# Building a graph adjacency matrix: who takes the window sums out of PSUM and adds them

## The reference, cut to what matters

```
dst = sorted(...)                       # 20000 destinations, denser at low numbers
count[s, d]     = sum over edges e of (src[e] == s) * (dst[e] == d)
adjacency[s, d] = sum over edges e of (src[e] == s) * (dst[e] == d) * edge_weight[e]
```

## Time and profile before

| | |
|---|---|
| median of 3 runs | 3178.88 us (3175.09 to 3182.57) |
| the profiled execution | 3182.64 us, its span 3180.9 us |
| mean granted TensorE clock | 0.901 |
| the stage `build_adjacency` | from 0 to 267.24 us, where the next stage's first load is issued |
| its windows | from 23.3 us on (first `first_hot`); TensorE's last matmul ends at about 252.65 us |

### The profile page before, as it was taken

How to read it: one execution, slowest core, us unless ns; L and a number is a source line. 1 busy time by engine, 2 the same in 40 slices (tenths; PEclk the granted TensorE clock), 3 DMA queues, 4 the chain that set the end, 5 groups by cost and what they waited for, 6 DMA issues and landing times. The chain is left out here.

```text
span 3180.9 us, 40026 instructions
## 1 busy us (share of the span) xinstructions
PE 2602.6 (82%) x14620; PEld 2308.1 (73%) x14621; DVE 2000.4 (63%) x2885; ACT 1356.1 (43%) x2206; POOL 358.5 (11%) x309
## 2 busy tenths in 40 slices
PE   5774878887986968984899779869897998999876
PEld 5663778887886868982788738457666776999766
DVE  7886278877967962225655444452796555899654
ACT  0343267575665641111566410031697102777430
POOL 1351030040031000000223201000000000111000
PEclk9996989998998979996999969979998997999978
DMA  0113101112111134211899770114552222443304
GB/s 33 25 39 85 48 23 44 50 44 66 41 52 38 57 108 102 48 35 43 281 245 249 197 155 0 49 72 148 147 122 51 60 86 49 98 102 86 92 1 102
DMA packets 107496, 268.23 MB, mean 84 GB/s; under 512 B 10934, under 2 KB 49320, under 8 KB 106346
## 3 DMA queue, kind: packets, MB, share of 16 engines
q1 hardware_dynamic: 99730, 239.43, 27.6%
q0 software_dynamic: 7616, 26.74, 3.9%
HBM read 195.58 MB, written 66.73 MB: 82 GB/s over the span
## 5 line engine op out<-in xcount | busy, mean ns | idle before, releaser
L888 PE MATMUL ps<-h,e_gat_aggregate 125*125 125x193 f32 x2400 | 408.9, 334 | 79.4 <-DVE e_gat_aggregate L872 63.3
L888 PEld LDWEIGHTS ps<-h,e_gat_aggregate 125*125 125x125 f32 x2400 | 402.3, 192 | 85.9 <-DVE e_gat_aggregate L872 66.8
L833 ACT ACTIVATE e_gat_aggregate<-row_gat_aggregate,from_src 125x1250 f32<-125x1250 f32 x120 | 160.7, 1339 | 155.7 <-PE ps L888 131.0
L870 DVE TENSOR_TENSOR e_gat_aggregate<-e_gat_aggregate 125x1250 f32<-125x1250 f32 x120 | 175.1, 1460 | 76.9 <-ACT e_gat_aggregate L836 76.9
L103 PE MATMUL ps<-gat_w_pair_gat_scores,x_turned 128*125 128x384 f32 x1080 | 196.3, 345 | 33.0 <-DVE gat_w_pair_gat_scores L748 33.0
L103 PEld LDWEIGHTS ps<-gat_w_pair_gat_scores,x_turned 128*125 128x125 f32 x1080 | 195.2, 191 | 33.9 <-DVE gat_w_pair_gat_scores L748 33.8
L103 PE MATMUL ps<-w_pair_dense_rows_from,col_dense_rows_from 128*125 128x384 f32 x1080 | 206.0, 349 | 1.8 <-DVE col_dense_rows_from L1024 1.8
L2366 DVE TENSOR_TENSOR ln_home<-p_attend,p_high_attend 125x1254 fp32r<-125x1254 f32 x120 | 184.4, 1550 | 27.9 <-ACT p_high_attend L2352 25.2
L103 PEld LDWEIGHTS ps<-w_pair_dense_rows_from,col_dense_rows_from 128*125 128x125 f32 x1080 | 195.1, 193 | 2.5 <-DVE col_dense_rows_from L1024 2.5
L2344 ACT ACTIVATE p_attend<-ps 125x1254 f32<-125x1254 f32 (+2 forms) x168 | 148.6, 915 | 80.2 <-PE ps L2307 79.3
L1859 DVE TENSOR_SCALAR_CACHE_REDUCE res_attention_statistics<-ps 125x1250 f32<-125x1250 f32 x120 | 173.1, 1459 | 11.4 <-PE ps L1836 5.1
(11 more groups left out here) (384 smaller groups left out, 5170.5 us busy)
## 6 DMA issues: line engine op xcount, KB each, us to landing
stock<-in_moe_w SPq DMA_DIRECT2D x34, 1152.0 KB
row_gat_aggregate<-r_scratch SPq DMA_DIRECT2D x24, 625.0 KB, 6.3
V_home<-q_scratch SPq DMA_DIRECT2D x44, 312.5 KB, 6.3
ln_home<-q_scratch SPq DMA_DIRECT2D x36, 312.5 KB
ln_home<-k_scratch SPq DMA_DIRECT2D x36, 312.5 KB
stock<-in_gat_w SPq DMA_DIRECT2D x4, 2304.0 KB, 8.8
rows_dense_rows_from<-node_scratch SPq DMA_DIRECT2D x8, 1080.0 KB
q_scratch<-V_home SPq DMA_DIRECT2D x6, 1250.0 KB, 4.5
```

Source lines behind the costliest of these rows:

```text
L833: a.activation(e[:, n % 3, 0, :], row[0:TP, head % 2, 0, :], ACT.Exp, bias=from_src[:, head, t:t + 1])
L870: v.tensor_tensor(e[:, n % 3, 0, :], e[:, n % 3, 0, :], e[:, n % 3, 1, :], ALU.max).then_inc(p_step, 1)
L888: last = pe.matmul(ps[0:TP, bank(head, d // 2), d % 2 * (C + 1):(d % 2 + 1) * (C + 1)], e[:, n % 3, 0, d * TP:(d + 1) * TP], h[:, t, head, :],
```

## The change

GpSimd's three instructions for each window go. ScalarE makes six copies for a window instead of three: for each bank, the three weight parts go to `stage` (now three kinds wide) and the counts go straight to `count` as 16-bit integers. VectorE does the two adds, two windows behind: while it works on window w, it adds part 0 and part 1 of window w-2 (`parts_sum`) between its two `first_hot` instructions, and adds part 2 (`adjacency`) behind them. For windows 0 and 1 the same instructions run on `stage` filled with zeros, which GpSimd now clears in the setup; the results for the windows "-2" and "-1" go to two additional windows at the front of `adj`, and the stores read it two windows further on. Behind the loop VectorE does the adds of windows 38 and 39.

```diff
--- before.py
+++ after.py
@@ -141,17 +141,19 @@
     half = ph.sb("weight_bf16", [TP, 2, 2, NP], BF16)
     nodes = ph.sb("node_iota", [TP, N], F16)
     dests = ph.sb("destination_iota", [TP, NPAD])
-    stage = ph.sb("window_sums", [TP, 2, NT, 4, WIN])
+    stage = ph.sb("window_sums", [TP, 2, NT, 3, WIN])
     src_hot = ph.sb("src_hot", [TP, 2, 2, N], BF16)
     dst_hot = ph.sb("dst_hot", [TP, 2, 4, WIN], BF16)
     first_hot = ph.sb("first_hot", [TP, 2, 4, WIN], BF16)
-    adj = ph.sb("adjacency", [TP, NT, NPAD])
+
+    LAG = 2
+    adj = ph.sb("adjacency", [TP, NT, NPAD + LAG * WIN])
     count, ident = g["count"], g["ident"]
     s = {n: ph.sem(n) for n in (
         "edges_in", "pool_step", "const_ready", "v_step", "ends_ready", "diag_done", "turned", "bounds_turned",
         "lohi_ready", "tables", "hot_ready0", "hot_ready1", "hot_free0", "hot_free1",
         "first_ready0", "first_ready1", "first_free0", "first_free1",
-        "staged", "ahead_in", "pool_sum", "window_out", "adj_stored")}
+        "staged", "ahead_in", "parts_sum", "stage_clear", "window_out", "adj_stored")}
     hot_ready = [s["hot_ready0"], s["hot_ready1"]]
     first_ready, first_free = ([s[f"{name}{j}"] for j in range(2)] for name in ("first_ready", "first_free"))
     hot_free = [s["hot_free0"], s["hot_free1"]]
@@ -176,7 +178,8 @@
             for first in range(0, NWIN, STORE):
                 sp.wait_ge(s["window_out"], first + STORE + 2)
                 here = slice(first * WIN, min((first + STORE) * WIN, N))
-                move_rows(sp, rows_out[:, :, here], adj[:, :, here], s["adj_stored"])
+                there = slice(here.start + LAG * WIN, here.stop + LAG * WIN)
+                move_rows(sp, rows_out[:, :, here], adj[:, :, there], s["adj_stored"])
             sp.wait_ge(s["adj_stored"], 32 * (NWIN // STORE))
             sp.wait_ge(s["ahead_in"], 16 * len(ahead))
 
@@ -187,6 +190,7 @@
             step(pool.affine_select(out=ident[:], in_=ident[:], compare_op=ALU.not_equal, fill=1.0, base=0,
                                     pattern=[[-1, 128]], channel_multiplier=1))
             pool.memset(ones[:], 1.0)
+            pool.memset(stage[:], 0.0)
             pool.memset(chain[:], 1.0)
             pool.iota(count_up[:], pattern=[[1, NWIN]], base=0, channel_multiplier=0, allow_small_or_imprecise_dtypes=True)
             pool.iota(words[:, 1], pattern=[[NP - 1, 3], [-2, NWIN // 2]], base=NP, channel_multiplier=0,
@@ -197,18 +201,6 @@
             pool.iota(dests[:], pattern=[[1, NPAD]], base=0, channel_multiplier=0, allow_small_or_imprecise_dtypes=True)
             step(pool.iota(nodes[:], pattern=[[1, N]], base=0, channel_multiplier=0, allow_small_or_imprecise_dtypes=True))
             pool.drain().then_inc(s["const_ready"], 1)
-
-            with pool.Fori(0, NWIN // 2) as i:
-                for odd in range(2):
-                    w = 2 * i + odd
-                    pool.wait_ge(s["staged"], w + 3)
-                    here = bass.ds(w * WIN, WIN)
-                    pool.tensor_copy(count[:, :, here], stage[:, odd, :, 0, :])
-                    pool.tensor_tensor(stage[:, odd, :, 1, :], stage[:, odd, :, 1, :], stage[:, odd, :, 2, :],
-                                       ALU.add).then_inc(s["pool_sum"], 1)
-                    pool.wait_ge(s["pool_sum"], w + 1)
-                    pool.tensor_tensor(adj[:, :, here], stage[:, odd, :, 1, :], stage[:, odd, :, 3, :],
-                                       ALU.add).then_inc(s["window_out"], 1)
 
         @block.vector
         def _(v):
@@ -293,6 +285,17 @@
                     value[:, j, c, :].rearrange("p a k -> p (a k)").unsqueeze(2).broadcast_to([TP, 4, WIN]),
                     ALU.is_equal, ALU.mult)
 
+            def parts_sum(odd, w):
+
+                v.wait_ge(s["staged"], w + 1)
+                v.tensor_tensor(stage[:, odd, :, 0, :], stage[:, odd, :, 0, :], stage[:, odd, :, 1, :], ALU.add).then_inc(s["parts_sum"], 1)
+
+            def adjacency(odd, w):
+
+                v.wait_ge(s["parts_sum"], w + 1)
+                v.tensor_tensor(adj[:, :, bass.ds(w * WIN, WIN)], stage[:, odd, :, 0, :], stage[:, odd, :, 2, :],
+                                ALU.add).then_inc(s["window_out"], 1)
+
             for j in range(2):
                 src_of(1, j, slice(0, 1))
             with v.Fori(0, NWIN // 2) as i:
@@ -303,12 +306,17 @@
                     for j in range(2):
                         v.wait_ge(first_free[j], w + 1)
                         dst_of(first_hot, j, bass.ds(first, 1), w).then_inc(first_ready[j], 1)
+                        if j == 0:
+                            parts_sum(odd, w)
+                    adjacency(odd, w)
                     with v.Fori(first + 1, pairs[odd + 1] + 1) as c:
                         for j in range(2):
                             v.wait_ge(hot_free[j], lead + c)
                             src_of(odd, j, bass.ds(c, 1))
                             dst_of(dst_hot, j, bass.ds(c, 1), w).then_inc(hot_ready[j], 1)
-            v.wait_ge(s["window_out"], NWIN + 2)
+            for odd in range(LAG):
+                parts_sum(odd, NWIN + odd)
+                adjacency(odd, NWIN + odd)
             for t in range(NT):
                 here = slice(t * TP, (t + 1) * TP)
                 last = v.tensor_tensor(count[:, t, here], count[:, t, here], ident[0:TP, 0:TP], ALU.add)
@@ -337,7 +345,6 @@
             for j in range(2):
                 pe.sem_inc(first_free[j], 1)
             pe.sem_inc(s["staged"], 2)
-            pe.sem_inc(s["window_out"], 2)
 
             def visit(two, hot, j, odd, opens):
                 for t in range(NT):
@@ -370,8 +377,9 @@
                     a.wait_ge(s["window_out"], w + 1)
                     for b in range(3):
                         n = 4 if b < 2 else 2
-                        last = a.activation(stage[:, odd, 4 * b:4 * b + n].rearrange("p t k d -> p (t k d)"),
-                                            ps[0:TP, 3 * odd + b, 0:n * 128], ACT.Copy)
+                        sums = ps[0:TP, 3 * odd + b, 0:n * 128].rearrange("p (t k d) -> p t k d", k=4, d=WIN)
+                        a.activation(stage[:, odd, 4 * b:4 * b + n], sums[:, :, 1:4, :], ACT.Copy)
+                        last = a.activation(count[:, 4 * b:4 * b + n, bass.ds(w * WIN, WIN)], sums[:, :, 0, :], ACT.Copy)
                     last.then_inc(s["staged"], 1)
     ph.end()
```

## The result

The median is 3174.07 us (3163.97 to 3180.17, 16 runs) against 3181.61 (3174.18 to 3189.25, 16 runs) for the kernel before on the same chip: a ratio of 0.9973, interval 0.9963 to 0.9983. By that ratio it is 8.6 us faster, between 5.4 and 11.8 (the medians themselves lie 7.5 apart). The profiled execution of after took 3175.12 us (span 3173.4). The forecast was 11.4 us.

What follows compares the result with a forecast made beforehand. No engine is full; the stage's window loop counts, its VectorE stretched by GpSimd. Loop -10.7 and -1.0, setup +1.7, end -1.35 sum to -11.35 us: 3178.9 - 11.4 = 3167.5 us, range 3157 to 3185.

Steps and rivals of the forecast that it cites:

- GpSimd's disturbance goes: Window loop: removing GpSimd's work ends stretched VectorE instructions; 22.6 us gained over 34 windows, bounds 19.9 to 25.4.
- the adds: VectorE, window loop: two adds of 0.49 us a window, costing 11.9 us over 34 windows, in odd windows only.
- setup: Before the first window: GpSimd clearing `stage` delays TensorE's first transposes, costing 1.7 us, bounds 0.8 and 1.9.
- end: Behind the last window: final sums no longer wait for GpSimd's queue, gaining 1.35 us.
- the pace formula: Window loop undisturbed: two windows with K chunks together take 1.85 K plus 2.55 us.
- the clock: TensorE, windows 8 to 37: lowered granted clock put at 2.8 us, taken off GpSimd's share of the 25.4 us.
- The cost of an odd window: VectorE, `first_hot` to `src_hot`: 1.65 us instead of 0.95 with the adds, so 0.70 us on the path.
- In even ones the slack of 1.04 hides it: Even windows: VectorE is ready 1.04 us before TensorE, so the adds' 0.70 us costs nothing there.
- VectorE is the bound in even windows too: Rival: all 40 windows pay 0.84 us for adds, 3187 us; slower from 0.63 us a window; chance of slower 14%.
- The register work of the adds' waits: Rival: odd windows pay 1.1 us instead of 0.70, giving 3175 to 3181 us; 23% together with late ScalarE.
- ScalarE is not late: Rival, one-chunk windows: six copies take 3.1 us, not 1.65, delaying VectorE; 3179 us; 23% together with register work.
- The adds are not hidden: Rival: adds nearly whole hidden at 0.43 us an odd window, giving 3162 us; chance 18%.

Runs made afterwards that it cites:

- e1: Kernel before without GpSimd's three instructions a window, ScalarE clearing the matrices in the setup: 3144.41 us, ratio 0.9892, loop 195.7 us.
- e9: Kernel before plus one small ScalarE copy ahead of the loop, so the function table loads once: 3178.05 us, ratio 0.9999, loop 236.4 us.
- e11: e1 with the changed kernel's six ScalarE copies a window, still no adds: 3143.32 us, ratio 0.9899, loop 196.6 us.
- e2: Changed kernel with both adds of every window replaced by one-element writes, waits and signals kept, ScalarE clearing the matrix: 3157.32 us, loop 208.3 us.
- e6: Changed kernel with `stage` cleared by two ScalarE copies instead of GpSimd's memset: 3170.1 us, ratio 0.9971, loop 224.8 us.
- e3: Changed kernel with the adds done in odd windows only: 3163.85 us in one execution, loop 215.9 us.
- e4: Changed kernel with the adds done in even windows only: 3164.15 us in one execution, loop 216.0 us.
- e8: Changed kernel with all stores held back until the last window is done: 3185.31 us in one execution, loop 219.5 us.
- e7: e6 with the four adds of two windows moved to the end of the loop's body: 3179.62 us, ratio 1.0002, loop 235.4 us.
- e10: e6 with four windows in one loop body instead of two: 3174.05 us, ratio 0.999, loop 221.1 us.

## Why the prediction was right, and what it had wrong

The sign held; the size came out smaller, and two terms of the sum were each wrong by more than the stage gained, in opposite directions. That the number came near is luck. In the stage they went as follows.

| term | forecast | measured |
|---|---|---|
| GpSimd's disturbance goes | -25.7 (22.6 + 1.0 + 2.1) | -35.1 (before to e1; -40.7 from e9) |
| six copies | 0 | +0.9 (e1 to e11) |
| waits and signals of the adds | in the next | +11.7 (e11 to e2) |
| the adds | +14.0 (11.9 + 2.1) | +18.0 (e2 to after; +16.5 to e6) |
| loop | -11.7 | -4.5 |
| setup | +1.7 | +1.63 |
| end | -1.35 | -1.6 |
| stage | -11.35 | -4.5 |

**The disturbance** was read rightly and priced too low, by 9.4 us. For windows 4 to 37 it is 30.2 us (the three stretches of the earlier trace rows less those of e1), against 22.6. Of the 7.6 missing, 4.8 are the pace formula, which was too slow for short windows, and 2.8 are the clock, which I had taken off as a cost of its own. The remainder lies in windows 0 to 3 and 38, 39 (4.9 us against 3.1). Nor is 35.1 a firm figure: e9, which differs from before by one small copy, had a loop 5.6 us longer, so the way in which GpSimd's adds happened to fall in the kernel before may be worth more than the whole gain. The Trainium skill, "SBUF — State Buffer", section "Who interferes with whom", holds that VectorE and GpSimd alone share a pair of ports and lock each other out of it; the trace agrees, as ScalarE's copies and the stores left the one-hots at 546 and 344 ns in after. In this loop 99 us of GpSimd's work cost 35.

**The cost of an odd window** was right in its form: 1.61 us from `first_hot` to `src_hot`, forecast 1.65. Against the undisturbed 0.93 of e1 it is 0.68, forecast 0.70.

**The cost of an even window is the step that failed.** "In even ones the slack of 1.04 hides it" rests on window 4 in the earlier trace rows, where VectorE's pause was 0.27 us. The trace of before shows that this window was no rule. Window 2 stands behind 7.9 us in which GpSimd did nothing (up to 63.44), and there it reads:

```profile
61.83 0.61 DVE L291 SCALAR_TENSOR_TENSOR irst_hot_build_adjacency<-ion_iota_build_adjacency,_columns_build_adjacency,e_values_build_adjacency 125x128 bf16 x2 [1.11 <-issue]
...
63.22 0.34 DVE L291 SCALAR_TENSOR_TENSOR dst_hot_build_adjacency<-ion_iota_build_adjacency,_columns_build_adjacency,e_values_build_adjacency 125x128 bf16 x1
...
63.74 0.74 PE L344 MATMUL ps<-dst_hot_build_adjacency,src_hot_build_adjacency 125*125 125x128 bf16 x10
```

The pause is 1.11, and TensorE comes 63.74 - 63.56 = 0.18 us behind `dst_hot`. In windows 8 to 14 of before the slack is 0.14, and only 6 of its 20 even windows have 0.9 or more. Why window 4 had a short pause was not tried by itself; shortly ahead of it stand two stretched instructions (0.91 at 75.48, and a `dst_hot` of 0.94 at 76.31), beneath which VectorE's own stream can have run on. If so, the slack was made by the very disturbance that the change removes. Undisturbed, the pause in windows 2 to 16 is 1.0 to 1.1 (e1) and the slack 0.17 to 0.30; e3 and e4 show that both parities pay alike, and e1 against e8 that each window pays 0.68. 40 windows at 0.68 are 27 us, where the runs show 29.7, with longer pauses beside the stores and a lower clock in it (e8). The rival "VectorE is the bound in even windows too" had the mechanism; its decision point of 0.63 us a window was passed. That the kernel is not slower is due to the other term: with a disturbance of 35.1 the point lies at (35.1 - 0.9 - 0.35) / 40 = 0.85.

**The signs named ahead.** Two windows of two chunks were to take 10.6 us instead of 11.4; they took 11.1 to 11.9 (windows 8 to 13), and TensorE waited for VectorE ahead of the first chunk in even windows too. The `first_hot` at 25.0 and adds of 0.49 us came.

**The other rivals.** The register work of the adds' waits is part of it: 0.22 us a window. ScalarE is not late: 2.7 us of waits at `parts_sum`, and the copies cost 0.9. The adds are not hidden.

**From the stage to the program.** The stage of the profiled executions gained 4.5 us, the median of the program 8.6 (5.4 to 11.8). The rest of the program, with the same code, took 3.1 us less in after's profile than in before's, but 4.6 more than in before's second profile. So the time beyond the stage's 4.5 can be chance of the rest or an effect of the change on it, and the profiles can't tell; it stays open. The forecast of 3167.5 was 6.6 below the median. Of that 2.7 is its starting point (3178.9 from three runs of before, 3181.6 from sixteen), and 3.9 is that the medians moved 7.5 and not 11.4.

## What to carry to other kernels

A slack read beside a disturbance belongs to the disturbance: before counting on it as cover, read it at a place that the disturbance doesn't reach, and look at more than one window. Work on GpSimd beneath a VectorE that sets the pace is not free even when GpSimd is idle most of the time; here two adds and a cast of 2.5 us a window cost VectorE's path 0.9 a window, as against 0.7 for the same adds done by VectorE itself. Two errors of the same sign in opposite terms can leave a forecast standing, so each term deserves a kernel of its own. And a kernel made to isolate one term has to be compared with one that differs in that term alone (e1 with e9, e2 with e6).

## What the runs showed of the hardware

- At the top of this hardware loop's body, where two windows' bounds are taken from one word in SBUF, VectorE pauses 1.0 to 1.1 us in the windows up to 16 and 0.7 or 1.1 in the shorter ones behind (e8); TensorE pauses 1.01. About 0.3 of it is gone behind a run of adds (e7) or where no jump stands (e10). While a store runs it grows to about 1.75 (after, e2), and without stores it doesn't (e8).
- TensorE's granted clock stayed at 1.00 in e8, where its idle stretches in the loop were at most 1.1 us, and in e1, with one of 1.49. In after there are four of 1.69 to 2.24 us. Behind the one of 1.69 the two next blocks took 2.27 and 2.00 us, 1.7 and 1.5 times the 1.34 of a block at 2.4 GHz; behind another, of 2.22, the next block took 1.34. An idle stretch of that length can cost the clock, but not each does. With 1.94 to 2.05 us at nearly every body the clock was 0.88 to 0.89 from 62 us on (e7).
- A wait and a signal around an instruction of one element cost VectorE 0.11 us each (e2: 0.22 a window for two).
- GpSimd can hold up VectorE with instructions that read nothing, one behind the other: the cast of the setup ended 0.27 to 0.28 us behind GpSimd's last iota in all fourteen profiled executions, and so took 2.85 us in after and 1.17 in e6.
